# Two transfers of the first FFN stage moved from SyncE's queue to those of ScalarE and GpSimd, and one wait of TensorE left out

## What is computed

```python
x = x + 0.5 * ffn(layernorm(x), k0, k1, k2, s0, s1, s2)
x = x + attn(layernorm(x), Wq, Wk, Wv, Wo, bo)
x = x + 0.5 * ffn(layernorm(x), k0, k1, k2, s0, s1, s2)

def ffn(x, k0, k1, k2, s0, s1, s2):       # weights are +1 where k is true, else -1
    h = concatenate([x, -x], axis=-1)     # 2048 features
    h = relu(s0 * (h @ sign(k0))) * 2     # k0: [2048, 4096] bool
    h = relu(s1 * (h @ sign(k1))) * 2     # k1: [4096, 4096] bool
    return s2 * (h @ sign(k2))            # k2: [4096, 1024] bool
```

## Time and profile before

| | |
|---|---|
| median of 2 runs | 3537.01 us (3446.96 and 3627.07) |
| profiled execution, its own time | 3447.69 us |
| its span (slowest core, core 5) | 3446.1 us |
| spans of the eight cores | 3423.2 to 3446.1 us |
| TensorE busy | 3046.8 us, 88% |
| VectorE busy | 532.4 us, 15% |
| ScalarE busy | 444.6 us, 13% |
| GpSimd busy | 169.0 us, 5% |
| bytes moved by DMA | 350.48 MB |

### The profile page before, as it was taken

One profiled execution on the slowest core, in us unless ns is written; L12 is line 12 of the kernel. 1 busy time (PEld: TensorE's weight loads), 2 busy tenths in 40 slices (PEclk: granted clock), 3 DMA queues, 4 the chain that ended last, 5 costly groups with the idle time before them and its releaser, 6 DMA issues.

```text
span 3446.1 us, 35806 instructions; the slowest of 8 cores (3423.2 to 3446.1 us)
## 1 busy us (share of the span) xinstructions
PE 3046.8 (88%) x14600; PEld 1398.3 (41%) x14600; DVE 532.4 (15%) x593; ACT 444.6 (13%) x745; POOL 169.0 (5%) x208
## 2 busy tenths in 40 slices
PE   0699999988999999974884759999999899999998
PEld 0244444433444444432433424444444344444443
DVE  2321111111000000134647540000000000000000
ACT  0121111100310000000214203111110031000000
POOL 0000000000000000000000000000000000000000
PEclk9999999999999999996995779999999999999999
DMA  9564645445232222437101252323223323231332
GB/s 142 117 180 129 184 127 164 130 147 171 74 98 61 86 74 74 141 107 150 25 1 31 91 169 80 107 60 108 68 89 98 117 67 98 61 98 56 91 98 98
DMA packets 223409, 350.48 MB, mean 102 GB/s; under 512 B 40720, under 2 KB 171792, under 8 KB 222992
## 3 DMA queue, kind: packets, MB, share of 16 engines
q0 software_dynamic: 79072, 191.91, 20.8%
q1 hardware_dynamic: 139424, 138.99, 13.6%
q10 hardware_dynamic: 4752, 17.30, 1.5%
HBM read 251.70 MB, written 83.89 MB: 97 GB/s over the span
## 4 chain that ended last, share of the span: by engine, by line
PE 79%; DMA 8%; DVE 7%; ACT 2%; issue 2%; another core or an unknown queue 1%; DVEq 0%; SPq 0%; ACTq 0%; POOL 0%; POOLq 0%
PE ps_b L511 29%; PE ps_a L511 22%; PE ps_b L571 6%; PE ps_b L445 6%; PE ps_a L445 5%; PE ps_a L571 5%; DMA sb<-k 2%; DMA sb<-k2pm_scr 2%; PE ps_b L699 1%; PE ps_t L310 1%; PE ps_b L967 1%; DMA xst<-x_scr 1%; ACT sb L811 1%; DVE sb L418 1%
## 5 line engine op out<-in xcount | busy, mean ns | idle before, releaser
L511 PE MATMUL ps_b<-sb 128*128 128x512 bf16 x4672 | 1301.0, 380 | 13.1 <-DVE sb L344 8.1
L511 PE MATMUL ps_a<-sb 128*128 128x512 bf16 x3520 | 1051.2, 379 | 9.9 <-DVE sb L344 4.9
L511 PEld LDWEIGHTS ps_b<-sb 128*128 128x128 bf16 x4672 | 457.2, 98 | 565.2 <-issue 22.4
L511 PEld LDWEIGHTS ps_a<-sb 128*128 128x128 bf16 x3520 | 344.5, 98 | 425.9 <-issue 16.5
L445 PE MATMUL ps_b<-sb 128*128 128x512 bf16 x1168 | 264.6, 385 | 70.2 <-DMA d_scr<-sb 70.1
L571 PE MATMUL ps_b<-sb 128*128 128x512 bf16 x1216 | 278.2, 390 | 44.0 <-DMA sb<-k2pm_scr 19.7
L445 PE MATMUL ps_a<-sb 128*128 128x512 bf16 x880 | 200.8, 385 | 21.4 <-DMA sb<-d_scr 17.3
L522 ACT ACTIVATE sb<-ps_b,deriv 128x512 bf16<-128x512 f32 x146 | 100.3, 687 | 911.6 <-PE ps_b L511 901.4
L445 PEld LDWEIGHTS ps_b<-sb 128*128 128x128 bf16 x1168 | 115.4, 99 | 212.7 <-issue 79.5
L571 PEld LDWEIGHTS ps_b<-sb 128*128 128x128 bf16 x1216 | 120.5, 100 | 199.7 <-issue 66.4
L571 PE MATMUL ps_a<-sb 128*128 128x512 bf16 x832 | 187.3, 387 | 15.6 <-DMA sb<-k2pm_scr 9.3
(11 more groups left out here) (93 smaller groups left out, 1012.2 us busy)
## 6 DMA issues: line engine op xcount, KB each, us to landing
sb<-k1pm_scr POOLq DMA_DIRECT2D x96, 1024.0 KB, 7.4
sb<-k POOLq DMA_DIRECT2D x40, 1024.0 KB, 6.0
k1pm_scr<-sb SPq DMA_DIRECT2D x32, 1024.0 KB, 9.3
sb<-d_scr SPq DMA_DIRECT2D x24, 1024.0 KB, 5.3
sb<-k2pm_scr POOLq DMA_DIRECT2D x24, 1024.0 KB, 7.8
x_scr<-sb SPq DMA_DIRECT2D x21, 512.0 KB, 2.6
sb<-x_in SPq DMA_DIRECT2D x19, 512.0 KB, 10.3
sb<-x_scr SPq DMA_DIRECT2D x19, 512.0 KB, 11.9
```

Source lines behind the costliest of these rows:

```text
L511: E.matmul(tile7[r], wst[:, qq, c3 % 8, nn * 128:(nn + 1) * 128], a1[:, c3, t2 * 512:(t2 + 1) * 512], start=(c3 == 0), stop=(c3 == 31)),
```

## The change

The load of the second byte tile goes from SyncE's queue to ScalarE's. The stash of d0 goes from SyncE's queue to GpSimd's. TensorE's matmul groups wait for the scaling alone and no longer for the stash. Later readers of the stash and of the slot still wait for it (`t_w_stash`, `slot_stash`).

```diff
@@ l0_half, in "if build and half == 0" @@
-                    tb = b.dma("sync", u8b[:],
+                    tb = b.dma("scalar", u8b[:],
                                k0_d[D:2 * D, nb * 512:(nb + 1) * 512]
                                .rearrange("(cc p) n -> p cc n", p=128),
                                reads=(u8_tok[1],))
@@
-                    st_["t_w_stash"] = b.dma("sync", d0blk, dsl, reads=(tslot,))
+                    st_["t_w_stash"] = b.dma("gpsimd", d0blk, dsl,
+                                             reads=(tslot,))
                     st_["slot_stash"][sl] = st_["t_w_stash"]
-                    tslot = (tslot, st_["t_w_stash"])
+                    tslot = (tslot,)
```

## The result

The changed kernel is slower. Runs of it and of the kernel before on the same chips give a ratio of 1.0291, with a 95% interval of 1.0257 to 1.0325. The plain medians, 3558.02 us for 11 runs and 3598.17 us for 10 of the kernel before, can't be compared: both sets hold runs in which a die had a lower clock (six of the ten of before), and the ratio leaves those out. The profiled execution of the changed kernel took 3541.8 us, that of the kernel before 3447.7, so 94 us more.

A forecast was written before the change was run, and what follows sets the result against it. Bound by a 49 us opening gap behind the W casts, then subtraction steps of 16.7 us. Serial 28.7 us steps and casts ahead of L1 outweigh the freed gap: 3447.7 + 106.9 + 2.8 = 3557 us, range 3518 to 3602.

The forecast's parts named there:

- the first L418: Opening of the first stage: VectorE's first subtraction of a k0 pair at 51 us, no longer held behind the W casts.
- u8b loads leaving ScalarE behind the eighth ReLU: Block loop before L1: each u8b load issues after the previous block's eight ReLUs, so load, subtraction and scaling follow the matmuls.
- casts behind the eighth stash: GpSimd's queue before L1: four W casts issued near 258 us instead of 4, landing 77 us later.
- one wait ahead of L1: Before L1's first matmul: TensorE stands some 73 us while the W casts hold back the first k1 load.
- 106.9 + 2.8 us: L1 starts 106.9 us later, at 348.0 instead of 241.1; TensorE's restart there at the lower clock adds 2.8.
- the term for all that follows the start of L1: From L1 on: same work and order in both kernels, only 2.8 us more for the lower clock.
- A step of the loop: Block loop before L1: 28.7 us from first matmul to first matmul against 16.7, counted seven times.
- The lone u8b load: In each block before L1: 5.3 us to landing, taken from the d0 load; possible 2.6 to 8.5.
- Idle ahead of each block: Block loop before L1: TensorE idle some 12 us before each block's matmuls.
- The casts: GpSimd's queue ahead of L1: four W casts at 19.4 us each, 77.6 us, landing at 342.5.
- The restart at L1: Start of L1: TensorE, after standing 73 us, starts at the lower clock, 2.8 us more.
- rival C: Opening: casts didn't hold the first k0 pair; first matmul at 105.6 instead of 56.9, 3606 us; chance 0.05.

## Why the prediction was right, and where it was wrong

**The mechanism, right.** Every sign that it named is in the trace: the first L418 at 50.3 (51 forecast), u8b loads leaving ScalarE behind the eighth ReLU, casts behind the eighth stash at 254 (258), one wait ahead of L1 of 73.7 us (73), ended by L344, and L1 at 342.5 (348.0). The expected 3557 us and its range of 3518 to 3602 hold all the runs that the ratio is formed from (3537.5 to 3563.8 us) and the median of all; the profiled execution lies 15 us under 3557.

**The base of the sum, the step that failed.** What failed is the step from the sum to the forecast. The prediction set its 106.9 + 2.8 us on one execution, 3447.7 us, and gave 3557 us and the range of 3518 to 3602 for that base alone. Read against the median that stood beside it, 3537.01, that is +0.6%; the measured ratio of 1.0291 is +2.9%, or 3640 us on that median, above the range. The prediction saw that the median was the mean of two runs far apart and gave 3.2% against the lower one, but it had no case in which that choice was wrong. The later runs show that the choice was right and the median no base: 3446.96 was the kernel's own time (3443.95, 3445.28 and 3449.49). On it, the ratio makes 3547 us, 10 under the forecast. So the change in per cent was right against the lower run and wrong against the median.

**The terms that were mis-sized.** The forecast had 109.7 us, the profiled executions differ by 94 and the mean spans by 98.5. The largest error is the term for all that follows the start of L1: 2.8 us more by the forecast, 3205.0 - 3197.7 = 7.3 less on the slowest cores.

- A step of the loop: 28.1 us against 28.7. The lone u8b load lands in 4.3 us in the median (5.3 taken, from the load of d0). Idle ahead of each block is 11.4 to 12.5 us (12). Seven steps make 4.4 us.
- The casts: (255.67 + 81.1 - 254.13 - 25.8) / 3 = 18.9 us for each after the first, against 19.4. The stash and the first cast together took 254.13 + 25.8 - 253.25 = 26.7, against 26.2.
- Together these make L1 5.5 us earlier than forecast. The other 10 us lie behind its start. From there to its end, core 5 of the kernel before, its slowest, took 3446.1 - 241.1 = 3205.0 us, while core 0 took 3433.2 - 235.8 = 3197.4 before and 3540.2 - 342.5 = 3197.7 after. I built on the slowest core's span as if that core would stay the slowest; in the changed kernel core 0 was last. That is 3205.0 - 3197.4 = 7.6 us.
- The restart at L1, put at 2.8 us, is the rest: on core 0 the two kernels differ by only 0.3 us from there on. L1's first line above shows the slower start (1.44 us for the first three matmuls, where the kernel before took 0.81). But the kernel before stands there for its second quarter of k1, 1.13 us on core 0, and the changed kernel, whose loads have landed, doesn't:

```profile
244.04 0.81 PE L511 MATMUL ps_b<-sb 128*128 128x512 bf16 x3 [1.13 <-DVE sb L344]
```

**The restarts in the loop, right.** The matmuls of block 1 take (97.39 + 3.62) - 84.58 = 16.4 us, as forecast. The granted clock falls in each gap, to 0.50 of 2.4 GHz, which is the 1.2 GHz level. Windows of the changed kernel at the start of block 1 and in the gap ahead of L1:

```profile
84.50:88.00 3.50, 3.42 (x9) 1.21 (x10) 0.00 (x0) 0.00 (x0) 0.91 (x1) 0.50 0.88 288
...
269.00:342.00 73.00, 0.00 (x0) 0.00 (x0) 2.04 (x3) 1.04 (x3) 3.20 (x4) 0.53 1.02 127
```

**The rule that the trace was at odds with.** The rule of the Trainium skill (page "DMA: Bandwidth & Descriptors", section "SWDGE vs HWDGE vs iDMA") that a DMA engine takes GpSimd's and the hardware-made queues in turn favoured rival C. The runs side with the landings: the first pair is at 51 us without the casts and at 98 with them, and a d0 load took 68 us among them. Only with 64 pieces did a load land before the last cast was issued, and it still took 56.6 us. The same page's section "Issuing engines are not separate DMA queues" says that starting transfers from several engines saves only the time to initiate them. On this the runs agree: the queue of the u8b load by itself brought nothing, its place in the order decided.

## What to carry to other kernels

A transfer that is moved to another engine's queue takes its place in that engine's program order: ask what stands ahead of it there, and what it now stands ahead of. Here the load waited for eight ReLUs that waited for the matmuls of the block before, and the stash pushed four casts with no deadline in front of the first load of the next stage. Transfers that nobody wants soon belong where the DMA engines have time; here, spread out between others in L1 of the second half, that alone was worth 1.7%, more than any edit to the loop.

## What the runs showed of the hardware

- DRAM-to-DRAM casts on GpSimd's queue hold back loads of SyncE's queue: 68.2 us to landing for 1 MB that takes 6.0, and 94.6 us for the first k0 pair. Cutting the casts into 16 changed nothing, into 64 took off 15 to 20 us (33 to 40 us of standing instead of 54 to 56).
- A lone load of 512 KB in pieces of 512 bytes lands in 4.2 to 4.3 us, on SyncE's queue as on ScalarE's, where a pair with a 1 MB stash in the same queue took 8.5.
- One cast of a 1024 x 1024 matrix from f32 to bf16, DRAM to DRAM, takes 19 us behind another one, for 6 MB read and written, at either end of the kernel's first 340 us. In that time a load of 1 MB, at its 6.0 us, could run three times.
